# Attention over a long context: the weighted sum is taken one head step later, behind the next head's transposes

## The reference

```python
q = x1 @ Wq                       # 128 x 1024
kv = x2 @ Wkv                     # 12544 x 2048
k, v = jnp.split(kv, 2, axis=-1)
q, k, v = map(_split_heads, (q, k, v))          # 16 heads of 64
attn = jnp.einsum('bhid,bhjd->bhij', q, k) * SCALE
attn = jax.nn.softmax(attn, axis=-1)
out = jnp.einsum('bhij,bhjd->bhid', attn, v)
return out @ Wo + bo
```

## Time and profile before

| what | us |
|---|---|
| median of three runs | 1564.63 |
| lowest and highest | 1563.09, 1567.99 |
| the profiled execution's own time | 1565.5 |
| its span, first to last instruction | 1563.8 |
| PE busy in the span | 1468.7 (94%) |
| PEld busy | 1303.5 (83%) |
| DVE busy | 1242.0 (79%) |
| ACT busy | 970.9 (62%) |
| POOL busy | 604.6 (39%) |

### The profile page before, as it was taken

The page is one execution under the profiler, slowest core; times in us unless marked ns, Lnnn a source line. Parts: engine busy times, 40 slices in busy tenths (PEclk is TensorE's granted clock), DMA queues, the critical chain, the costliest instruction groups (busy, mean ns, idle before and its releaser), DMA issues. The chain is left out here.

```text
span 1563.8 us, 24194 instructions
## 1 busy us (share of the span) xinstructions
PE 1468.7 (94%) x8657; PEld 1303.5 (83%) x8657; DVE 1242.0 (79%) x2278; ACT 970.9 (62%) x1807; POOL 604.6 (39%) x519
## 2 busy tenths in 40 slices
PE   6999999999999999999999999999977989999479
PEld 5988998899889888988898889889865878888248
DVE  6888888888888888888888888888975356666764
ACT  4777777777777777777777777777651245555121
POOL 6334343434343434343434343433300256665330
PEclk9999999999999999999999999999997899999779
DMA  5000000000000000000000000000007122220600
GB/s 182 1 1 25 1 25 1 24 1 24 1 25 1 25 1 25 1 25 1 25 1 25 1 25 1 1 1 1 1 28 296 74 72 70 70 70 24 282 1 4
DMA packets 9099, 57.13 MB, mean 37 GB/s; under 512 B 2120, under 2 KB 2719, under 8 KB 7968
## 3 DMA queue, kind: packets, MB, share of 16 engines
q1 hardware_dynamic: 8992, 55.73, 9.6%
HBM read 55.60 MB, written 0.13 MB: 36 GB/s over the span
## 5 line engine op out<-in xcount | busy, mean ns | idle before, releaser
L314 POOL CAST V<-Vraw 128x512 fp32r<-128x512 f32 x189 | 115.8, 613 | 654.4 <-ACT Vraw L405 654.4
L369 ACT CAST K<-ps 64x448 fp32r<-64x448 f32 x448 | 236.4, 528 | 142.6 <-PE ps L532 133.1
L397 ACT ACTIVATE pT<-ps 128x896 fp32r<-128x896 f32 x224 | 206.3, 921 | 161.9 <-PE ps L558 161.7
L435 DVE TENSOR_TENSOR K<-ps,K 64x448 fp32r<-64x448 f32 x448 | 278.8, 622 | 13.3 <-ACT K L369 3.4
L493 DVE TENSOR_TENSOR pT<-ps,pT 128x896 fp32r<-128x896 f32 x224 | 244.6, 1092 | 31.9 <-ACT pT L397 8.3
L315 POOL TENSOR_TENSOR V<-Vraw,V 128x512 fp32r<-128x512 f32 x189 | 242.2, 1281 | 15.2
L443 DVE TENSOR_REDUCE nmx<-ps 128x1 f32<-128x896 f32 x224 | 242.2, 1081 | 0.0
L643 PEld LDWEIGHTS ps<-pT,V 128*128 128x128 f32 x1568 | 214.3, 189 | 17.0 <-DVE pT L493 7.5
L643 PE MATMUL ps<-pT,V 128*128 128x256 f32 x1568 | 222.5, 281 | 6.1 <-DVE pT L493 6.1
L379 ACT ACTIVATE prob<-ps,nm 128x896 f32<-128x896 f32 x224 | 224.3, 1001 | 0.0
L602 PE MATMUL ps<-ident,prob 128*128 128x128 f32 x1568 | 209.0, 274 | 0.0
(11 more groups left out here) (306 smaller groups left out, 2389.9 us busy)
## 6 DMA issues: line engine op xcount, KB each, us to landing
raw<-in_ctxT SPq DMA_DIRECT2D x14, 896.0 KB, 4.7
d_raw<-in_ctxT SPq DMA_DIRECT2D x14, 896.0 KB, 4.6
w<-in_w SPq DMA_DIRECT2D x2, 4096.0 KB, 16.8
wg<-in_wg SPq DMA_DIRECT2D x1, 4352.0 KB, 25.7
wu<-in_wu SPq DMA_DIRECT2D x1, 4352.0 KB, 16.8
wd<-in_wd SPq DMA_DIRECT2D x1, 4352.0 KB, 26.7
e_ea<-in_alog SPq DMA_DIRECT2D x1, 2048.0 KB, 7.3
wq<-in_wq SPq DMA_DIRECT2D x1, 1024.0 KB, 5.2
```

The source lines that it names most:

```text
L369: nc.scalar.copy(K[halves[s], slot, cols], ps[halves[s], piece_bank(p), 0:HK]).then_inc(sem("kh_ready"), 1)
L397: nc.scalar.activation(pT[:, :, 0, :], pT_ps, ACT.Copy).then_inc(sem("pTh_ready"), 1)
L435: ins = nc.vector.tensor_tensor(K[halves[1 - s], slot, cols], ps[halves[s], piece_bank(p), 0:HK], K[halves[s], slot, cols].bitcast(F32), A ...
```

## The change

It does these things, all in `stage_context`.

- `weighted_sum(u - 1)` now stands in step `u`, behind the transposes of step `u` and `turn_sums(u - 2)`. For that `pT` has two buffers, and the transposes of step `u` wait for `pTl_ready` of step `u - 1`.
- PE makes the key piece before the value piece; the value piece is last in the step, and it now also waits for `o_added`, since the weighted sum of the step before lies in its bank.
- ACT copies `Vraw` of step `u - 1` first in step `u`, ahead of the turned probabilities.
- DVE writes the low key parts first, then adds the halves, then writes the low part of the turned probabilities. `update_sums` runs two steps behind. The row maximum stands ahead of `den`. `scale_sums` runs in odd steps from `u = steps - 13`, before it was even steps from `steps - 14`.
- Behind the loop stand the last `turn_sums`, the last `weighted_sum` and the turned heads.
- A set of small tiles for later stages is allocated after this stage and not before it, which makes the room for the second `pT`. Their loads stand where they stood.

```diff
-        pT = sb("pT", [P, NT, 2, P], F32R, keep)
+        pT = [sb(f"pT{i}", [P, NT, 2, P], F32R, keep) for i in range(2)]
...
                 for u in range(steps):
-                    act.wait_ge(sem("p_turned"), u + 1)
-                    nc.scalar.activation(pT[:, :, 0, :], pT_ps, ACT.Copy).then_inc(sem("pTh_ready"), 1)
-                    if u + 1 < steps:
-                        exp_step(u + 1)
-                    if u in v_steps:
-                        j = v_steps.index(u)
+                    if u - 1 in v_steps:
+                        j = v_steps.index(u - 1)
                         act.wait_ge(sem("v_done"), NT + j + 1)
                         if j >= 2:
                             act.wait_ge(sem("v_split"), j - 1)
                         nc.scalar.copy(Vraw[:, j % 2, :], ps[:, 6, :]).then_inc(sem("vraw_ready"), 1)
+                    act.wait_ge(sem("p_turned"), u + 1)
+                    nc.scalar.activation(pT[u % 2][:, :, 0, :], pT_ps, ACT.Copy).then_inc(sem("pTh_ready"), 1)
+                    if u + 1 < steps:
+                        exp_step(u + 1)
...
-                    dve.wait_ge(sem("p_turned"), u + 2)
+                    dve.wait_ge(sem("p_turned"), u + 3)
...
+                    if 1 <= u and u - 1 + AHEAD < steps:
+                        low_parts(u - 1 + AHEAD)
                     if u >= 1:
                         add_parts(u - 1)
-                        if u - 1 + AHEAD < steps:
-                            low_parts(u - 1 + AHEAD)
                     dve.wait_ge(sem("pTh_ready"), u + 1)
...
-                    if u >= 1:
-                        update_sums(u - 1)
+                    if u >= 2:
+                        update_sums(u - 2)
+                    if u + 2 < steps:
+                        max_step(u + 2)
...
-                    if u + 2 < steps:
-                        max_step(u + 2)
-                    m = (u - (steps - H0)) // 2 - 1
-                    if u > steps - H0 and u % 2 == 0:
-                        scale_sums(m)
+                    if u >= steps - H0 + 3 and u % 2 == 1:
+                        scale_sums((u - (steps - H0) - 3) // 2)
+                update_sums(steps - 2)
                 add_parts(steps - 1)
...
+                def weighted_sum(u):
+                    h, g = u % H0, u // HG
+                    pe.wait_ge(sem("pTl_ready"), u + 1)
+                    if u in v_steps:
+                        pe.wait_ge(sem("vraw_ready"), v_steps.index(u) + 1)
+                    if h % HG == 0:
+                        if g == 0:
+                            pe.wait_ge(sem("first_vl"), NT)
+                        else:
+                            pe.wait_ge(sem("v_split"), NT * g)
+                    for k in range(NT):
+                        mm = nc.tensor.matmul(OT_ps, V[g % 2][:, k, h % HG, :],
+                                              pT[u % 2][:, k, :, :].rearrange("p a q -> p (a q)"),
+                                              start=(k == 0), stop=(k == NT - 1))
+                    mm.then_inc(sem("pv_done"), 1)
...
                     pe.wait_ge(sem("exp_done"), u + 1)
-                    if u >= 2:
-                        pe.wait_ge(sem("u_added"), u - 1)
+                    if u >= 1:
+                        pe.wait_ge(sem("pTl_ready"), u)
+                    if u >= 3:
+                        pe.wait_ge(sem("u_added"), u - 2)
...
+                    if u >= 2:
+                        mm = turn_sums(u - 2)
+                    mm.then_inc(sem("p_turned"), 1)
                     if u >= 1:
-                        mm = turn_sums(u - 1)
-                    mm.then_inc(sem("p_turned"), 1)
+                        weighted_sum(u - 1)
...
+                    p = u + AHEAD
+                    if p < steps:
+                        if p == AHEAD:
+                            pe.wait_ge(sem("first_vl"), NT)
+                        pe.wait_ge(sem("kl_ready"), p)
+                        piece(p)
                     if u in v_steps:
...
+                        if u >= 1:
+                            pe.wait_ge(sem("o_added"), u)
...
+                pe.wait_ge(sem("u_added"), steps - 2)
+                turn_sums(steps - 2).then_inc(sem("p_turned"), 1)
+                weighted_sum(steps - 1)
+                turn_heads((4, 5, 6), 7)
+                pe.wait_ge(sem("u_added"), steps - 1)
```

More of the change, by code:

```diff
@@ L96, in build @@
         keep("zero", [P, 1])
[L97 to L107, removed]
         def norm_vector(dve, n):
@@ L136, in build @@
         stage_context(nc, t, sb, sem, link, ps, norms, v)
+        keep("wg0", [P, KT, E0])
+        keep("bg", [P, E0])
+        keep("b2", [E0, D])
+        keep("wx", [P, KT, D])
+        keep("bx", [P, KT])
+        keep("wxp", [P, KT, DTR + 2 * NST])
+        keep("wdt", [DTR, D])
+        keep("bdt", [1, D])
+        keep("dskip", [P, D])
+        keep("wr1", [P, KT, E1])
+        keep("br1", [P, E1])
         with ExitStack() as experts:
@@ L487, in _ @@
                     h, b = u % H0, u % 4
+                    if 1 <= u and u - 1 + AHEAD < steps:
+                        low_parts(u - 1 + AHEAD)
                     if u >= 1:
                         add_parts(u - 1)
-                        if u - 1 + AHEAD < steps:
-                            low_parts(u - 1 + AHEAD)
                     dve.wait_ge(sem("pTh_ready"), u + 1)
-                    nc.vector.tensor_tensor(pT[:, :, 1, :], pT_ps, pT[:, :, 0, :].bitcast(F32),
+                    nc.vector.tensor_tensor(pT[u % 2][:, :, 1, :], pT_ps, pT[u % 2][:, :, 0, :].bitcast(F32),
                                             ALU.subtract).then_inc(sem("pTl_ready"), 1)
-                    if u >= 1:
-                        update_sums(u - 1)
+                    if u >= 2:
+                        update_sums(u - 2)
+                    if u + 2 < steps:
+                        max_step(u + 2)
                     if u >= H0:
@@ L621, in _ @@
                         values(gn, i, 6)
-                    p = u + AHEAD
-                    if p < steps:
-                        if p == AHEAD:
-                            pe.wait_ge(sem("first_vl"), NT)
-                        pe.wait_ge(sem("kl_ready"), p)
-                        piece(p)
                     if u == steps - 1:
@@ L633, in _ @@
                         project(range(0, 4))
-                    pe.wait_ge(sem("pTl_ready"), u + 1)
-                    if u in v_steps:
-                        pe.wait_ge(sem("vraw_ready"), v_steps.index(u) + 1)
-                    if h % HG == 0:
-                        if g == 0:
-                            pe.wait_ge(sem("first_vl"), NT)
-                        else:
-                            pe.wait_ge(sem("v_split"), NT * g)
-                    for k in range(NT):
-                        mm = nc.tensor.matmul(OT_ps, V[g % 2][:, k, h % HG, :],
-                                              pT[:, k, :, :].rearrange("p a q -> p (a q)"),
-                                              start=(k == 0), stop=(k == NT - 1))
-                    mm.then_inc(sem("pv_done"), 1)
                     if u == steps - 3:
@@ L649, in _ @@
                         turn_heads((0, 1, 2, 3), 7)
-                    if u == steps - 1:
-                        turn_heads((4, 5, 6), 7)
+                pe.wait_ge(sem("u_added"), steps - 2)
[3 more added lines that the diff above has]
+                pe.wait_ge(sem("u_added"), steps - 1)
                 turn_sums(steps - 1).then_inc(sem("p_turned"), 1)
```

## The result

| | before | after |
|---|---|---|
| median of 9 runs each, us | 1565.05 | 1568.86 |
| lowest and highest | 1561.96, 1567.99 | 1566.62, 1571.48 |
| ratio, 95% interval | | 1.0035 [1.0018, 1.0052] |
| profiled execution: own time, span | 1565.5, 1563.8 | 1568.74, 1566.9 |

By this ratio the change makes the kernel slower by 0.35%. The interval leaves out no change, but it does not leave out 0.3%, which the prediction took as the least that can be told from no change. The two medians themselves lie 3.8 us, 0.24%, apart. The time lies 2.9 us above the predicted 1566.0, inside the range of 1554 to 1580. It is just inside the likeliest case as it was written, "1560 to 1569", and by the ratio just beyond the 0.3% that this case stood for.

The account below looks back on a forecast made before the run. The prediction took PE to bound the long stage, with DVE next. Its terms, 24.6 + 5.9 - 22.1 - 2.8 - 4.5 = +1.1 us on a span of 1563.8, gave a median of 1566, range 1554 to 1580.

Parts of the forecast that it names:

- the likeliest case: Whole kernel: the stalls cancel and the time is 1560 to 1569 us; chance 0.44.
- The stall at the weighted sum: PE waits for ACT's value copy in bank 6: 0.13 us in each of 189 steps, 24.6 us.
- The rival of the hidden wait: Weighted sum's copy wait hidden or cheap: cost 0 to 13.2 us, time 1541 to 1554; chance of faster 0.26.
- The 0.86 a group: Most that better order returns per eight steps, 40.43 against 39.57 us; 0.82 taken, 22.1 us over 27 groups.
- The new wait of the transposes for the low probabilities: At the transposes after a short step: not felt, load can start at 3.68 and is due at 3.76 us.
- The short step: Step without a value piece, last in a group of eight: lasts 3.86 us with the 0.13 us stall.
- The border wait of the key piece: Key piece after a short step waits for DVE's low key parts: 0.22 us in 27 groups, 5.9 us.
- The end of the stage: Last four recurrences of L493, 20.5 us before: 4.5 us less taken, between 2.5 and 5.9.
- the ring: Last four recurrences: transposes, weighted sum, halves, low parts in a cycle of 3.65 us a step, 14.6 for four.
- The divisions' stalls: Last 16 steps: L558's 0.95 us wait in three steps with divided heads goes, 2.8 us gained.
- The longer wait: Weighted sum's copy wait is longer, deciding from 0.15 us a step: 1575 at 0.18, 1585 at 0.23; chance 0.25.
- The change doesn't do what it says: Short step stays 4.12 us, the next 5.5, as DVE's round of 4.4 exceeds 3.73: 1582 us; chance 0.05.

Follow-up runs that it names:

- experiment 1: Changed kernel with the weighted sum's two waits exchanged, so the value-copy wait lies on the matmul itself: 1559.32 us, ratio 0.9966 to the kernel before.
- experiment 2: Changed kernel with ACT's copy of the value piece made in four instructions of 128 columns: 1602.21 us in one run.
- experiment 3: Changed kernel with PE's scores ahead of the weighted sum and DVE's low probabilities ahead of the added halves: 1552.6 us, ratio 0.9922.
- experiment 4: Changed kernel with the transposes' wait for u_added moved from the first to the fifth transpose: 1569.61 us, ratio 1.0031.
- experiment 8: Changed kernel, scores before weighted sum, latest waits first, u_added at fifth transpose, cast wait split per low_parts, den of steps without value piece deferred one step: 1544.40 us.
- experiment 9: Changed kernel, scores before weighted sum, latest waits first, later u_added, split cast wait, deferred den, row maximum over half the scores in short steps: 1537.48 us.
- experiment 10: Kernel before with only DVE edits: each low_parts waits for its own half of the cast, den of short steps done one step later: 1560.84 us, ratio 0.9974.
- experiment 7: Changed kernel, scores before weighted sum, latest waits first, u_added at fifth transpose, each low_parts waiting for its own half of the cast: 1550.10 us, ratio 0.9917.
- experiment 6: Changed kernel with DVE's row maximum reading only half of the scores in steps without a value piece: 1567.02 us, ratio 1.0018.
- experiment 11: Kernel before with only scale_sums moved to the odd steps where the change puts it: 1561.21 us in one run.

## Why the prediction was right and where it was wrong

**The stall at the weighted sum was right** in place, cause and size. The copy starts 0.20 behind the transposes, the load comes 0.11 behind its end, PE stands still 0.135 us in a full step, 0.13 foretold. Experiments 1 to 3 show it three times: 0.06 less by a cheaper restart, 0.18 more by a longer copy, gone behind the scores. The rival of the hidden wait fell: even with the wait on the matmul itself the load starts only when the copy is done (86.09, 86.14). The rule of the Trainium skill that it leaned on ("TensorE: Matmul & The Clock Gate", the table at the top) speaks of loads pulled ahead of matmuls in flight. The trace agrees where nothing waits (load at 60.30, product at 60.50 in the kernel before); what fell is the reading that a load would also pass an open wait.

**The 0.86 a group to be had back was too much.** The step that failed is "seven full steps and one short one without waits would be 7 x 5.12 + 3.73 = 39.57". 5.12 stands on one step; six in a row take 30.8 / 6 = 5.13. So the group without waits is 39.66, 0.77 below 40.43, and the two waits, 0.78, were all there was. I took 0.82: 0.04 x 27 = 1.1 us too much. (Here and below a group without waits is 39.66.)

**A wait was missed.** "The new wait of the transposes for the low probabilities is not felt: these end at 2.48 + 1.09 = 3.57, the load can start at 3.68": that is so, but the same transposes also wait for `u_added`, and DVE adds into `U` behind the low probabilities. In the profile this ends 81.11 - 79.76 = 1.35 after the low probabilities' start; with the prediction's own 2.48 it is 3.83, and the load at 3.94 where 3.76 was due. The short step takes 3.98 where 3.86 was foretold, and 3.73 + 0.135 is 3.87 with the stall as measured: 0.11 x 27 = 3.0 us. This is the largest error of the groups. Experiment 4 shows that the wait exists, and also that it cannot be cured by itself.

**The border wait of the key piece was right:** 0.22 foretold. The step behind the short one takes 5.33, 0.20 over a full step without waits; in the mean of the groups, 40.87 - 39.66 - 7 x 0.135 - 0.11 leaves 0.16 for it. With 0.16 it costs 1.6 us less than was foretold in 27 groups, and the stall, 0.135 for 0.13, 0.9 more.

**The end of the stage gave more.** The last four recurrences take 15.0 us; 14.6 was the ring worked out, 16.0 what I took, because of the clock. The granted clock stayed at 1.00 there, the 2.4 GHz level, where the kernel before had 0.85 over its own last four:

```profile
1151.60:1172.30 20.70, 13.78 (x74) 11.24 (x74) 12.42 (x30) 8.89 (x18) 0.00 (x0) 0.85 0.00 1
```

PE did the same 74 matmuls in both stretches, in 13.78 us there and in 10.04 here. So 5.5 us were gained for 4.5. The ring is 3.75 and not 3.65 a step, again by the addition into `U`: where its wait stands later (experiment 4) it is 14.2 / 4 = 3.55. How much of this the clock gives differs from trace to trace: the kernel of experiment 1 has the same ring, and its last four take 16.1 us at a granted clock of 0.91.

The divisions' stalls gave the 2.8 foretold: steps 207 to 215 lost 43.2 - 40.4 = 2.8 against a usual group before, and lose nothing now (40.87 both). Between the last recurrence and the end of the stage another 1.8 us fell away (4.5 behind becomes 2.7), and the prediction had no term for it. It is the clock again. In both kernels the last weighted sum stands behind the first eight matmuls of the output projection; the first row is from the kernel before, the second from the changed one:

```profile
1172.33 3.78 PE L568 MATMUL ps<-wo,oT 128*128 128x256 f32 x8
```

```profile
1176.88 1.99 PE L583 MATMUL ps<-wo,oT 128*128 128x256 f32 x8
```

They took 1.79 us longer at a granted clock of 0.50, the 1.2 GHz level, than at 1.00. In the kernel before PE had been busy for 5.99 of the 10.4 us from 1151.6 to 1162 at 1.00, and the clock was lower from there to 1175.5 (0.72, 0.69 and 0.50 in three stretches); in the changed one it was busy for 10.04 of 15.10 and the clock stayed. What keeps it up is not shown, and other runs of the changed kernel may differ: this trace has the highest mean clock of its nine runs (0.976, the others 0.972 to 0.973).

**Sum.** In the 27 groups +12.0 for the +8.4 foretold (24.6 + 5.9 - 22.1), and at the end -10.1 for -7.3 (2.8, 5.5 and 1.8). That makes +1.9 of the span's +3.1; of the rest 0.6 lies before the first step, 0.2 between step 215 and the last four, and 0.4 behind the stage. The groups were 3.6 worse than foretold and the end 2.8 better, so it is partly luck that the total came out closer than its terms.

**The rivals.** The longer wait (from 0.15 a step) did not come. That the ratio says slower all the same is due to other terms: the missed wait alone, 3.0 us, is as much as the 2.9 between forecast and result. "The change doesn't do what it says" fell: the turned sum never waits. Its reason, that DVE's round of 4.4 us exceeds the short step of 3.73, was nearer than its chance of 0.05: it doesn't keep the old waits, but it sets what is left of them, as experiments 8 to 10 show.

## What to carry to other kernels

When a consumer is moved nearer to a transfer that it shares a bank with, count from the block's start to the copy's end plus the restart, and multiply by the steps: a stall of 0.13 us, in no list of waits and with PE "busy" 100%, ate a whole improvement. In this program, where the first wait in the code is the one that lies on the matmul, put the wait that is fulfilled last first, or put 0.8 us of other work between. And go through every semaphore ahead of a moved instruction, not only the one that is new: where two come ready within 0.1 us, the cure of one shows nothing (experiment 7) or next to nothing (experiments 4 and 6), and can still be worth something together with the other (experiments 8 and 9).

## What the runs showed of the hardware

- A matmul's load follows the other engine's end by 0.05 us when the wait lies on the matmul and by 0.11 when it lies in an instruction of its own ahead of it (experiment 1; in 7 steps of every 8, some 10 us in all). "Advanced Engine Details and Errata", section Sequencer Loop, of the Trainium skill says that a control instruction starts executing in the sequencer's own code, but also that other engine instructions can be read and queued meanwhile. So it does not by itself give a reason for the 0.06, and no run here shows one.
- A copy of 512 columns out of PSUM takes 0.59 us in one ACT instruction and 0.77 in four of 128 columns (experiment 2), that is 0.06 for each more. A single copy of 128 columns out of PSUM takes 0.27 (L414 in the kernel before, at 1179.73).
- DVE's addition over two finished heads takes 1.25 us when it meets POOL's L315 and 0.27 when it does not (experiment 11, three and five of eight in the kernel before). In the changed kernel all eight take at most 0.275:

```profile
L463 DVE TENSOR_TENSOR U<-U x8: 269/272/275, 1124.1 to 1181.2; 128x128 f32<-128x128 f32 x8
```
